# One VectorE instruction for two row maxima, where their PSUM banks are neighbours

## The reference, cut to what matters

```
q = q.reshape(b, HEADS, HEAD_DIM, t)
k = k.reshape(b, HEADS, HEAD_DIM, s)
v = v.reshape(b, HEADS, HEAD_DIM, s)
dot = jnp.einsum('bhdt,bhds->bhts', q, k) / math.sqrt(HEAD_DIM)
mask = target_mask[:, :, :, None] * source_mask[:, :, None, :]
dot = mask * dot - (1.0 - mask) * NEG
amap = jax.nn.softmax(dot, axis=-1) * mask
out = jnp.einsum('bhts,bhds->bhdt', amap, v)
```

## Time and profile before

| | us |
|---|---|
| median of 3 runs | 1266.68 |
| the runs | 1265.74 to 1266.74 |
| the profiled execution | 1268.15 |
| its span, first to last instruction | 1266.3 |

### The profile page before, as it was taken

How to read it: one execution, slowest core, us unless ns; L and a number is a source line. 1 busy time by engine, 2 the same in 40 slices (tenths; PEclk the granted TensorE clock), 3 DMA queues, 4 the chain that set the end, 5 groups by cost and what they waited for, 6 DMA issues and landing times. The chain is left out here.

```text
span 1266.3 us, 14046 instructions
## 1 busy us (share of the span) xinstructions
PE 1089.0 (86%) x4802; PEld 424.1 (33%) x4802; DVE 1033.0 (82%) x1568; ACT 672.6 (53%) x787; POOL 515.0 (41%) x403
## 2 busy tenths in 40 slices
PE   4977689999999999778999976999999997189586
PEld 2543112222222222134444433444444443134232
DVE  5679779999999999378999964887888888776898
ACT  1655148888888888946566652110000000786896
POOL 2765221535435436520101014878888883000021
PEclk9989569999999999999999996999999999599889
DMA  9799852446446444132111101121211110000011
GB/s 325 246 306 334 258 181 93 131 129 200 119 141 195 129 146 121 49 122 109 34 51 49 35 20 46 56 64 53 67 54 62 61 55 17 1 1 1 9 59 66
DMA packets 74215, 132.89 MB, mean 105 GB/s; under 512 B 18848, under 2 KB 37664, under 8 KB 73632
## 3 DMA queue, kind: packets, MB, share of 16 engines
q1 hardware_dynamic: 74144, 132.00, 32.4%
HBM read 107.58 MB, written 22.02 MB: 102 GB/s over the span
## 5 line engine op out<-in xcount | busy, mean ns | idle before, releaser
L821 DVE TENSOR_REDUCE mneg<-ps_m 128x1 f32<-128x512 f32 x512 | 324.9, 683 | 38.2 <-PE ps_m L738 34.2
L1383 PE MATMUL ps_y<-kv,toeplitz_sb 128*128 128x512 f32 x640 | 280.4, 597 | 9.8 <-POOL kv L1295 9.8
L696 ACT ACTIVATE probs<-ps_s 128x1024 f32<-128x1024 f32 x256 | 250.7, 1023 | 39.7 <-PE ps_s L760 39.6
L1383 PEld LDWEIGHTS ps_y<-kv,toeplitz_sb 128*128 128x128 f32 x640 | 121.4, 192 | 156.7 <-issue 156.7
L760 PE MATMUL ps_s<-qk_stack 128*128 128x512 bf16 x512 | 138.9, 386 | 23.2 <-ACT probs L696 17.5
L738 PE MATMUL ps_m<-qk_stack 64*128 64x512 bf16 x512 | 126.0, 411 | 14.5 <-DMA qk_stack<-mask_k 12.5
L770 PE MATMUL ps_o<-probs,v_all 128*17 128x512 f32 x1024 | 135.6, 602 | 0.2 <-ACT probs L696 0.2
L1295 POOL TENSOR_TENSOR kv<-vT,ctxT_sb 128x2048 f32<-128x2048 f32 x32 | 118.7, 3710 | 41.2 <-PE ps_y L1383 33.4
L1001 PE MATMUL ps_g<-w,xT_f 128*128 128x512 bf16 x512 | 119.3, 382 | 11.4 <-DVE h_f L1167 7.9
L1449 DVE TENSOR_TENSOR z<-ps_y,ctxT_sb 128x1024 f32<-128x1024 f32 x64 | 77.9, 1217 | 48.1 <-PE ps_y L1383 48.1
L1348 ACT ACTIVATE w_anchor<-w_f 128x512 f32<-128x512 f32 x32 | 20.1, 628 | 180.6 <-DMA w_f<-in_w 180.6
(11 more groups left out here) (159 smaller groups left out, 1624.7 us busy)
## 6 DMA issues: line engine op xcount, KB each, us to landing
qk_stack<-qk_parts SPq DMA_DIRECT2D x192, 128.0 KB, 4.0
w_sweep<-in_w SPq DMA_DIRECT2D x8, 1536.0 KB, 10.9
qk_parts<-qk_part SPq DMA_DIRECT2D x48, 256.0 KB, 4.6
w_sweep<-in_w SPq DMA_DIRECT2D x16, 768.0 KB, 5.2
w_sweep<-in_w SPq DMA_DIRECT2D x16, 512.0 KB, 3.7
toeplitz_sb<-in_toeplitz SPq DMA_DIRECT2D x32, 256.0 KB, 2.6
w_f<-in_w SPq DMA_DIRECT2D x32, 256.0 KB, 2.9
v_rows<-vp SPq DMA_DIRECT2D x8, 544.0 KB, 10.3
```

What stands on the lines that cost most here:

```text
L696: nc.scalar.activation(pr[:, k % 2, 2 * slot:2 * slot + 2, :], S[:, 2 * slot:2 * slot + 2, :], ACT.Exp).then_inc(exp_done, 1)
L821: nc.vector.tensor_reduce(mneg[:, h, tc, hd:hd + 1], M[:, bank(j), :], AX.X, ALU.max, negate=True).then_inc(max_red, 1)
L1383: mm = nc.tensor.matmul(Y[:, q % 3, l2, :], T[:, g % 2, (lt - m) * P:(lt - m + 1) * P], kv[:, g % 2, m, :], start=(m == 0), stop=(m == lt))
```

## The change

`reduce_some` takes the tiles of a step two by two. Where the second one's bank follows the first one's in PSUM (banks 0 and 1, or 1 and 2), it waits for the later of the two matmuls and issues one reduction that reads both banks, 1024 values per row, and writes the two maxima; at its end it adds 2 to `max_red`. Where the banks are 2 and 0, `reduce_tile` is called twice as before. PE's instructions and waits stay as they are.

```
+    def reduce_some(dve, v, h, some):
+
+        for i in range(0, len(some), 2):
+            (tile, j), (second, k) = some[i:i + 2]
+            if bank(k) == bank(j) + 1:
+                dve.wait_ge(max_mm, TILES * v + second + 1)
+                a, hd, tc = place(tile)
+                nc.vector.tensor_reduce(mneg[:, h, tc, hd:hd + QUAD + 1:QUAD], M[:, bank(j):bank(j) + 2, :],
+                                        AX.X, ALU.max, negate=True).then_inc(max_red, 2)
+            else:
+                reduce_tile(dve, v, h, tile, j)
+                reduce_tile(dve, v, h, second, k)
...
-        for tile in range(HALF):
-            reduce_tile(dve, 0, 0, tile, HALF + tile)
-        for tile in range(HALF, TILES):
-            reduce_tile(dve, 0, 0, tile, tile - HALF)
+        reduce_some(dve, 0, 0, [(tile, HALF + tile) for tile in range(HALF)])
+        reduce_some(dve, 0, 0, [(tile, tile - HALF) for tile in range(HALF, TILES)])
...
-        for tile in range(HALF):
-            reduce_tile(dve, 1, 1, tile, HALF + tile)
+        reduce_some(dve, 1, 1, [(tile, HALF + tile) for tile in range(HALF)])
...
-                    for ahead, tile, j in tiles(k, more, not last):
-                        reduce_tile(dve, u + ahead, (h + ahead) % 2, tile, j)
+                    some = tiles(k, more, not last)
+                    if some:
+                        ahead = some[0][0]
+                        reduce_some(dve, u + ahead, (h + ahead) % 2, [x[1:] for x in some])
```

## The result

| | before | changed |
|---|---|---|
| median, us | 1266.21 (4 runs) | 1318.62 (4 runs) |
| the runs, us | 1264.89 to 1266.74 | 1318.25 to 1322.41 |
| ratio to before, 95% interval | | 1.042 (1.0407 to 1.0432) |
| span of the profiled execution, us | 1266.3 | 1316.9 |
| granted clock, mean | 0.937 | 0.94 |

The change makes the kernel 4.2% slower, by 52.4 us. Slower was forecast, at 1305.4 us with a range up to 1316; the loss is 13 us larger than the forecast and 2.6 us beyond the range.

What follows compares the result with a forecast made beforehand. PE was taken to set the pace, DVE only looking full. A loss of 2.7 us per unit over fourteen periods gives 37.8 us, plus 0.9 makes 38.7; on the median of 1266.68 that is 1305.4 us, range 1294 to 1316.

Steps and rivals of the forecast that it cites:

- Rivals 1: DVE is the resource that counts and fewer instructions help: gain 11.4 us, to 1255.2 us; chance 0.03.
- 2: The stops are absorbed by PE's and ACT's other waits, time within 0.2%; chance 0.04.
- 3: PE, interrupted in the loop, loses its clock (0.50 instead of 1.00), about 1415 us; chance 0.03.
- 4: A fused instruction costs 0.2 us more than one of 1024 elsewhere: another 2 us per unit, 1335 us; chance 0.03.
- slot 3: In step 1, the stop is given back because the second scores wait 0.78 us for ACT anyway: -0.4 us per unit.
- slot 15: PE already waits there because a statistics instruction held DVE up, so the stop adds only +0.06 us per unit.
- the turn: Turn of the maxima (slots 19, 20, 21): its 0.30 us wait for DVE goes, other waits change, together 0.
- The start: First maxima, ahead of the scores: +4.8 us, hidden in the wait for mrow's transfer with about 0.2 us to spare.
- +0.9: First unit's last two steps at full clock, before 185.4 us: two full stops and the small one, +0.9 us.
- 0.04 (to DVE): Time from the end of a pair's matmuls to DVE's start, in the 1.71 us chain to the next second matmul.
- the eight places that pay in full: Fused pairs whose second slot is 23, 27, 29, 1, 3, 7, 9, 13: 0.40 us stop each, +3.2 us per unit.
- The bounds: Fused reduction 1.21 to 1.30 us, response 0.04 to 0.08: 2.4 to 3.3 us per unit, 1301 to 1314; below, 1295.

Runs made afterwards that it cites:

- fuse_slot0: Changed kernel with only the pair at slots 0 and 1 fused, one of 11: 1266.8 us, ratio 1.0004 to the kernel before.
- fuse_slot4: Changed kernel with only the pair at slots 4 and 5 fused, one of 11: 1273.42 us, ratio 1.0058 to the kernel before.
- late_both: Changed kernel with two single reductions per fused pair, the first waiting for the second matmul, both banks released after the second: 1318.27 us, ratio 1.0409 to before.
- late_release: Changed kernel with two single reductions per fused pair, each started by its own matmul, both banks released after the second: 1299.77 us, ratio 1.0266 to before.
- fuse_inc1: Changed kernel with each fused reduction adding 1 to max_red instead of 2, waits recounted: 1310.72 us, ratio 1.0352 to the kernel before.
- wait_second: Changed kernel with two single reductions per fused pair, released one by one, the first also waiting for the second matmul: 1266.22 us, ratio 1.0004 to before.
- swap_halves: wait_second with the two halves of the PE array exchanged between a pair's matmuls: 1267.44 us in one execution.
- forms: wait_second with three other forms of the first reduction, one each at slots 4, 10 and 24 (sums not the reference's): 1273.32 us in one execution.

## Why the prediction was right or wrong

- **PE sets the pace, DVE only looks full.** Right. With less work on DVE the loop got longer, and in `fuse_slot0`, where PE's one stop is given back, the DVE time saved changed nothing. Rivals 1 and 2 are out; so is 3, the clock stays at 1.00 in the loop; and 4, the fused instruction takes 1.226 us.
- **The fused pair stops PE at the second matmul of the next pair.** Right, place by place: `fuse_slot4` costs one stop of 0.50 us per unit, and `late_both` shows the whole loss with no fused instruction.
- **What gives stops back** (slot 3, slot 15, the turn) was right in kind and nearly in size: 0.78 to 0.30 at slot 3 (0.48 for the forecast's 0.4), +0.11 at slot 15 for 0.06, the turn's wait gone. The forecast had the pair behind the turn held by about 0.2; it is not held at all. The start was hidden, though barely. The +0.9 forecast for the stage from the first scores to the first split of the loop can't be told: it took 16.2 us for 15.3, but with a clock that rose 2.2 us earlier.
- **The term that failed is the "0.04 (to DVE)" of the chain**, 0.39 + 0.04 + 1.22 + 0.06 = 1.71. I took it from a reduction that waits for the first matmul of its pair and carries its own wait. The fused one starts 0.137 us after a pair and 0.106 after a matmul alone. So the eight places that pay in full cost 4.0 us and not 3.2. 0.069 of each is the separate wait instruction that comes with adding 2: 0.58 us a unit (26.69 to 26.11), 8 us in all. 0.034 is the later signal of the second of two matmuls that end together. It counts only behind a pair that was not held itself, at five of the eight places (slots 23, 27, 1, 7, 13), so about 0.2 us a unit; that is worked out, not shown by a run of its own. 2.7 + 0.58 + 0.2 makes the measured 3.5 (26.69 less 23.18).
- **The bounds** were also summed too tight. A reduction of 1.30 us and a response of 0.08 together lengthen the chain by 0.12 us; at eight places less the one given back that is 0.84 on the 2.7, so 3.5 a unit and some 1317 us, not 3.3 and 1314. The measured response of 0.106 to 0.137 us lies outside even so: its bounds were drawn around the value of a like row, when the row was not like: it had another wait and another signal.
- **Open:** two of the fourteen periods of the changed kernel last 27.04 in place of 26.69 us. In each of them one fused reduction (at 231.41 and at 501.77 us) starts 0.40 us after the end of its semaphore instruction, where it is 0.04 elsewhere, and the next pair is held 0.35 us longer. Why it started late the trace doesn't show.
- Of my expectations, `late_release` was off by 12 us: I had treated each pair's stop as independent of how the next pair starts.

## What to carry to other kernels

Here a ring of three buffers, emptied in twos, stopped its producer wherever the producer had no other wait to hide it. Before merging two reads, ask when the first buffer is due back, and measure against the producer's next need, not against the consumer's busy share. Work of a consumer that looks full was free where the producer waited for something else anyway, and cost in full one slot later; moving 0.68 us of it per unit gained 4.3 us in all, shortening it by 0.06 gained nothing. If a merged instruction must signal, let it add 1 and change the counts: that was worth 8 us here.

## What the runs showed of the hardware

- A DVE reduction that adds 2 to its semaphore does not carry its wait: a semaphore instruction of 21 ns stands ahead of it, and it starts 0.069 us later after the event (0.137 against 0.068, 0.106 against 0.037). With 1 the difference is gone (`fuse_inc1`), and a single reduction that adds 2 has the instruction too (`late_release`).
- After two matmuls on the two halves of the PE array that end within 2 to 5 ns, a DVE instruction that waits for the second starts 0.034 us later than one that waits for the first, whichever half is second (`wait_second`, `swap_halves`).
- A DVE reduction over two PSUM banks costs nothing for the second bank: 0.691 us for 512 elements from two banks against 0.692 from one (`forms`). 1024 elements from two banks with two outputs take 1.226 us, and when it adds 1 its start is that of the single form.
